# Two attention projections by Strassen's seven block products, with the banks, buffers and schedule around them rebuilt

## The reference, cut to what matters

```
q = xn @ wq            # 32 heads; of each head's 192 columns the first 128 are used
k = xn @ wkv[:, :32*128];  v = xn @ wkv[:, 32*128:64*128]
scores = where(causal, (q_h . k_h) * 192**-0.5, -1e30)     # per batch row, sequence 128 or 256
attn   = softmax(scores) @ v_h ;   x += attn.reshape(..) @ wo
x += xn @ W_base.T + b_base + experts(xn)
```

## Time and profile before

| | |
|---|---|
| median of 3 runs | 1168.38 us (1167.16 to 1169.59) |
| the profiled execution | 1166.81 us, span 1165.1 us |
| granted TensorE clock, mean over the span | 0.996 |
| VectorE busy | 514.5 us (44%), 1409 instructions |
| ScalarE busy | 402.9 us (35%) |
| GpSimd busy | 491.2 us (42%) |
| HBM read | 56.50 MB, 50 GB/s |

### The profile page before, as it was taken

How to read it: one execution, slowest core, us unless ns; L and a number is a source line. 1 busy time by engine, 2 the same in 40 slices (tenths; PEclk the granted TensorE clock), 3 DMA queues, 4 the chain that set the end, 5 groups by cost and what they waited for, 6 DMA issues and landing times.

```text
span 1165.1 us, 18048 instructions
## 1 busy us (share of the span) xinstructions
PE 1149.5 (99%) x6014; PEld 986.4 (85%) x6014; DVE 514.5 (44%) x1409; ACT 402.9 (35%) x1215; POOL 491.2 (42%) x623
## 2 busy tenths in 40 slices
PE   8989999999999999999999999999999999999998
PEld 7767888898888888888888888888888888888887
DVE  6776256275344334334433443344234423443345
ACT  2321132012363236224513451355135413532451
POOL 3655497671354136323623351346135512642330
PEclk9989999999999999999999999999999999999999
DMA  6312322130011002000200030112011100110001
GB/s 207 106 57 84 126 90 72 46 113 28 19 64 37 28 18 72 27 27 18 90 9 27 18 99 0 36 44 64 0 36 56 52 27 18 63 36 28 10 1 73
DMA packets 24814, 59.00 MB, mean 51 GB/s; under 512 B 3536, under 2 KB 3856, under 8 KB 24656
## 3 DMA queue, kind: packets, MB, share of 16 engines
q1 hardware_dynamic: 24784, 58.61, 15.6%
HBM read 56.50 MB, written 2.10 MB: 50 GB/s over the span
## 4 chain that ended last, share of the span: by engine, by line
PE 94%; DVE 4%; ACT 1%; issue 0%; DMA 0%; SPq 0%; POOL 0%; DVEq 0%; ACTq 0%; POOLq 0%
PE banks L100 28%; PE banks L102 28%; PE banks L101 28%; PE banks L1189 4%; PE banks L1204 2%; PE banks L1180 2%; DVE acc L1113 1%; PE banks L708 0%; DMA acc<-in_x 0%; DVE work L417 0%; PE banks L832 0%; DVE s L488 0%; DVE hT_lo L445 0%; DVE s L487 0%; DVE work L442 0%
## 5 line engine op out<-in xcount | busy, mean ns | idle before, releaser
L1003 POOL TENSOR_SCALAR prob<-prob,inv 128x128 f32<-128x128 f32 x128 | 48.0, 375 | 544.5 <-DVE inv L1090 544.5
L100 PE MATMUL banks<-xT_hi,wqk_hi 128*128 128x512 f32 x512 | 208.0, 406 | 0.0
L102 PE MATMUL banks<-xT_hi,wqk_lo 128*128 128x512 f32 x512 | 200.1, 391 | 0.0
L101 PE MATMUL banks<-xT_lo,wqk_hi 128*128 128x512 f32 x512 | 199.6, 390 | 0.0
L1062 ACT ACTIVATE prob<-prob,top 128x128 f32<-128x128 f32 (+1 forms) x256 | 114.6, 449 | 192.8 <-DVE top L1100 192.8
L102 PEld LDWEIGHTS banks<-xT_hi,wqk_lo 128*128 128x128 f32 x512 | 96.1, 188 | 21.5
L101 PEld LDWEIGHTS banks<-xT_lo,wqk_hi 128*128 128x128 f32 x512 | 96.5, 189 | 17.1
L100 PEld LDWEIGHTS banks<-xT_hi,wqk_hi 128*128 128x128 f32 x512 | 96.2, 188 | 16.8
L1033 DVE TENSOR_TENSOR kT_lo<-banks,kT_hi 128x512 fp32r<-128x512 f32 x64 | 44.3, 692 | 140.9 <-ACT kT_hi L1028 140.9
L100 PE MATMUL banks<-wv_hi,xT_hi 128*128 128x512 f32 x256 | 103.4, 404 | 0.0
L100 PE MATMUL banks<-wo_hi,oT_hi 128*128 128x512 f32 x256 | 101.6, 397 | 0.0
(11 more groups left out here) (225 smaller groups left out, 2488.6 us busy)
## 6 DMA issues: line engine op xcount, KB each, us to landing
wqk_stage<-in_w_qk SPq DMA_DIRECT2D x32, 512.0 KB, 3.3
gu_stage<-in_w_gu SPq DMA_DIRECT2D x22, 512.0 KB, 3.3
wvo_stage<-in_w_v SPq DMA_DIRECT2D x32, 256.0 KB, 2.6
wvo_stage<-in_w_o SPq DMA_DIRECT2D x32, 256.0 KB, 2.6
wd_stage<-in_w_down SPq DMA_DIRECT2D x22, 256.0 KB, 2.7
acc<-in_x SPq DMA_DIRECT2D x8, 256.0 KB, 4.8
out<-acc SPq DMA_DIRECT2D x8, 256.0 KB, 2.0
tab<-in_w_comb SPq DMA_DIRECT2D x1, 1300.0 KB, 6.2
```

The costliest lines, as they stand in the source:

```text
L100: nc.tensor.matmul(out, w_hi, x_hi, start=first, stop=False)
L101: nc.tensor.matmul(out, w_hi, x_lo, start=False, stop=False)
L102: return nc.tensor.matmul(out, w_lo, x_hi, start=False, stop=last)
L1003: nc.gpsimd.tensor_scalar(prob[:, i, 0:P], prob[:, i, 0:P], inv[:, i, 0:1], 1.0, ALU.mult, ALU.mult)
```

## The change

The weights of a head's queries and keys, side by side, are a matrix of 512 features by 256 columns; the tokens are 512 by 1024. Both are cut into 2 x 2 blocks (features in two halves; queries and keys; tokens in two halves) and the product is formed by Strassen's scheme in Winograd's form: seven block products instead of eight, each of 2 x 3 matmuls of 512 columns into one bank (`product`). So a head has 42 matmuls of 512 columns where it had 48.

What comes with it:
- Once, at the end of layer 0: sums and differences of the token blocks (`mix`, four VectorE instructions of 128x256 for each of four tiles), their hi (ScalarE, 128x1024, `mixed_evac`) and lo (GpSimd, 128x1024), and a copy `xh` of the first half's transposed tiles (ScalarE, four times). VectorE's `mix` of tile 2 waits for GpSimd's lo of tile 0 (two buffers), and `linear_add(3)` stands behind all four mixes. SP now issues the first two attention loads as soon as the convolution is done (`y_done`).
- For each head on GpSimd (`prepare`): the key weights times 8 (`K_UNIT`), four sums or differences (S1 to S4, 128x256) and seven splits of 128x256 (hi and lo), instead of four instructions of 128x512.
- For each head on VectorE (`combine`): seven additions of 128x512, each of one SBUF and one PSUM operand; four of them write back to their PSUM bank, from which ScalarE and VectorE then take hi, full copy and lo as before. ScalarE copies the first product out of PSUM (`copy_p1`).
- The copy v_full moves from VectorE to ScalarE.
- W covers two heads instead of four: twice the units of 6 matmuls, and 128 additions to `acc` in all where there were 72.
- Banks: four of the products rotate over banks 0 and 1, all else over 2, 6 and 3; the transposes of a pair go into its score bank. Buffers oT and wo hold two heads; alignment of some buffers is 512 bytes instead of 2048.
- The first group is written out as well as the last; the loop runs over six.
- Less runs ahead inside layer 0: six of head 0's seven products in place of Q, K and two V.

The diff, cut to its core (the lists that give the order, the preparation of the weights, the combination, and layer 0's end):

```diff
-GBANKS = 4
+P1, P6, P2, P7, P4, P5, P3 = range(7)
+EVACUATED = P2, P4, P5, P3
+def with_pairs(slots, first=False):
+    for p, fill in enumerate(slots):
+        older = [] if first and p == 0 else [p - 1]
+        steps += [("S", p)] + [("T", n) for n in older] + [("X", p)] + fill[:1] + [("R", p)] + fill[1:]
+        steps += [("O", n) for n in older]
+MIDDLE_SLOTS = [
+    [("L", 0, P5), ("P", 0, P3), ("V", 4), ("L", 0, P3), ("Y", 4), ("P", 1, P1), ("W", 0, 0)],
+    [("P", 1, P6), ("V", 5), ("P", 1, P2), ("W", 0, 1), ("L", 1, P2)],
...
+    [("W", 0, 4), ("W", 0, 5), ("L", 1, P5), ("P", 1, P3), ("W", 0, 6), ("W", 0, 7)]]
+INNER_SLOTS = [
+    [("P", 2, P1), ("L", 1, P3), ("P", 2, P6)],
+    [("P", 2, P2), ("L", 2, P2), ("P", 2, P7)]]
+OUTER_SLOTS = [
+    [("P", 2, P4), ("W", 1, 0), ("L", 2, P4), ("P", 2, P5), ("W", 1, 1)],
...
+    [("L", 2, P3), ("P", 3, P6), ("W", 1, 4), ("P", 3, P2)],
+    [("L", 3, P2), ("P", 3, P7), ("W", 1, 5), ("P", 3, P4)],
+    [("L", 3, P4), ("W", 1, 6), ("P", 3, P5)],
+    [("L", 3, P5), ("P", 3, P3), ("W", 1, 7)],
+    [("P", 4, P1), ("L", 3, P3), ("P", 4, P6)],
+    [("P", 4, P2), ("V", 8), ("L", 4, P2), ("P", 4, P7), ("Y", 8), ("V", 9)],
+    [("P", 4, P4), ("V", 10), ("L", 4, P4), ("P", 4, P5), ("Y", 10), ("V", 11)]]
+SPLITS = [
+    forms(1, [P2, "S4", P7, P4]),
+    forms(1, [P5, P3]) + forms(2, ["scale", "S1", P1]),
...
+    forms(2, [P4, P5]) + WV[0:2],
+    WO[0:2],
...
+        def mix(t):
+            b1, b2 = banks[:, D + t, 0:2 * P], banks[:, D + t, 2 * P:4 * P]
+            a1, a2 = xh[:, t, 0:2 * P], xh[:, t, 2 * P:4 * P]
+            dve.wait_ge(xh_done, t + 1)
+            if t >= 2:
+                dve.wait_ge(mixed_ready, t - 1)
+            link(nc.vector.tensor_tensor(t1, b1, a1, ALU.subtract))
+            link(nc.vector.tensor_tensor(t2, b2, t1, ALU.subtract))
+            nc.vector.tensor_tensor(t3, t2, a1, ALU.subtract)
+            nc.vector.tensor_tensor(t4, a2, t2, ALU.subtract).then_inc(x_mixed, 1)
...
-        for t in range(TH, NT):
-            xT_evac(NT + t, D + t - TH)
-        for n in range(2, TH):
-            linear_add(n)
+        for t in range(TH):
+            xT_evac(NT + TH + t, D + t)
+            mix(t)
+            if t % 2:
+                linear_add(2 + t // 2)
         gates(0)
...
-        ahead(0, 1)
+        ahead(0)
         gated_transposes(0)
-        ahead(1, 2)
+        ahead(1)
         experts(0)
         gated_transposes(1)
-        ahead(2, 3)
+        ahead(2)
         experts(1)
-        ahead(3, 4)
+        ahead(3)
...
+    def combine(dve, g, steps, h, i):
+        bank = turn_bank(steps, ("P", h, i))
+        dve.wait_ge(prod_done, products(g, h, i))
+        if i == P6:
+            dve.wait_ge(p1_copied, g * GH + h + 1)
+            nc.vector.tensor_tensor(u2[:, :], u3[:, :], bank, ALU.add).then_inc(mix_done, 1)
+        elif i == P2:
+            nc.vector.tensor_tensor(bank, u3[:, :], bank, ALU.add).then_inc(mix_done, 1)
...
+    def product(pe, g, h, i, bank):
+        pe.wait_ge(form_ready, g * (GH * NP) + h * NP + i + 1)
+        for c in range(FT):
+            ins = matmul3(nc, bank, form_hi[:, i, c], form_lo[:, i, c],
+                          right[0][:, k0 + c, cols], right[1][:, k0 + c, cols], c == 0, c == FT - 1)
+        ins.then_inc(prod_done, 1)
```

More of the change, by code:

```diff
@@ L98, in matmul3 @@
+LAST_SPLITS = [[task for task in slot if task[0] != "wv" and (task[0] == "wo" or task[1] < GH)] for slot in SPLITS]
+PIECES = WV[0:2] + WO[0:2] + WV[2:4] + WO[2:4]
+LAST_PIECES = WO
+RING = 2
+WARM_UP = 17, 10
 def matmul3(nc, out, w_hi, w_lo, x_hi, x_lo, first, last):
@@ new lines, in attention, with groups, head, products @@
+    late_wo = tT_hi[:, 0:PAIRED], tT_lo[:, 0:PAIRED]
+    def groups(eng, body):
+        body(0, FIRST)
+        with eng.Fori(1, NG - 1) as g:
+            body(g, MIDDLE)
+        body(NG - 1, LAST)
+    def head(g, h):
+        return g * GH + h
+    def products(g, h, i):
+        return g * (GH * NP) + h * NP + i + 1 + PROD0
+    def mixes(g, h, m):
+        return g * (GH * NM) + h * NM + m + MIX0
+    def pieces(g, i):
+        return g * len(PIECES) + i + 1 + KD
+    def w_count(g, steps, step):
+        before = 0 if steps is FIRST else g * (2 * NT) - NT
+        return before + adds(steps).index(step) + 1
@@ new lines, in turn_bank, with o_part @@
+    def turn_bank(steps, step):
+        long = is_long(step)
+        own, taken = turns(steps, long)
+        ring = LONG if long else SHORT
+        return banks[:, ring[(taken.index(step) - (len(taken) if steps is FIRST else own)) % len(ring)]]
+    def o_part(steps, n):
+        h, half = n // BATCH, n % BATCH // 2
+        cols = slice(half * HALF, (half + 1) * HALF)
+        if steps is LAST and h >= PAIRED:
+            return late_oT[0][:, h % PAIRED, cols], late_oT[1][:, h % PAIRED, cols]
+        return oT_hi[:, h % PAIRED, cols], oT_lo[:, h % PAIRED, cols]
@@ new lines, in split_piece, with gpsimd_ahead @@
+    def split_piece(pool, i, hi, lo, count):
+        nc.gpsimd.tensor_scalar(hi, wvo_stage[:, i % RING], 1.0, 1.0, ALU.mult, ALU.mult).then_inc(vo_hi_done, 1)
+        pool.wait_ge(vo_hi_done, count)
+        nc.gpsimd.tensor_tensor(lo, wvo_stage[:, i % RING], as_f32(hi), ALU.subtract).then_inc(vo_ready, 1)
+    def gpsimd_ahead(pool, part):
+        if part == 0:
+            for what in HEAD_BEGIN:
+                prepare(pool, 0, 0, what)
+            return
+        for what in HEAD_END:
+            prepare(pool, 0, 0, what)
```

716 lines of the change are left out of this document (437 added, 279 removed), and 11 rows, old and new, of tables (GROUP, LAST_GROUP, START).

## The result

The changed kernel takes **1159.41 us** (median of 4 runs, 1157.67 to 1159.94) where the kernel before takes 1168.68 beside it: a ratio of 0.9918, 95% interval 0.9906 to 0.9931. It is faster by 9.3 us; the forecast was 24.6. The profiled execution is that of 1157.67, its span 1155.8 us.

A forecast was written before the change was run, and what follows sets the result against it. TensorE, busy 99% of the span, was taken as the bound. Terms -43.7 + 5.6 + 11 + 1.5 + 1 = -24.6 us on 1166.8, or 1143.8 against the median of 1168.4; range 1133 to 1155.

The forecast's parts named there:

- over 17: Sign of a wrong prediction: the meeting of the layers costs under 6 or over 17 us.
- What is removed, and the prices added: 192 matmuls at 0.2275 us, 43.7 us off TensorE; added per group: VectorE 22.0 us, GpSimd to 77, ScalarE to 48.
- 0.8 us per group: Looped groups' short slots: late VectorE and GpSimd chains delay transposes, 0.8 us in each of seven groups, 5.6 in all.
- The clean case: Rival: bank and pair chains in groups fit as now, the layers' meeting costs 6 us; 1131 us, chance 0.22.
- steps 1 to 3: Where the layers meet: late biases, slow mixes and slow second gates make TensorE lose 9 to 14 us.
- I take 11: Where the layers meet: the value chosen for TensorE's waits, 11 us from a range of 9 to 14.
- step 1: Layers' meeting: GpSimd prepares six tasks of head 0 ahead of the four biases, which end at 246.4, not 242.1.
- the price of the mixes: Layers' meeting: 1.7 us per tile free, 2.6 beside GpSimd; linear_add(3) at about 257, TensorE loses 5.5 us.
- Step 3: Layers' meeting: second gates slow beside GpSimd, TensorE has 2.7 us of products as cover; it loses 3.4 to 8.3 us.
- I add 1.5 here: Layers' meeting: lower granted clock about and after gaps, 1.5 us, from 3.4 us seen at a 5.7 us gap.
- I add 1: Tail: W(2,0) waits 0.7 us for oT_lo(13), W(2,4) 0.1 for oT_lo(15); 1 us added.
- the case of late chains: Rival: 2.7 us lost per group and the full 14 + 1.5 + 1 elsewhere; 1160 us, chance 0.13.

The follow-up runs named there:

- experiment 11: Changed kernel with unused filler matmuls in TensorE's three gaps where the layers meet, no wait shortened: 1154.37 us, ratio 0.9878 to the kernel before.
- experiment 1: Changed kernel with the mixes' second term kept in PSUM, so no subtraction has two SBUF operands: 1157.3 us, ratio 0.9913 to the kernel before.
- Experiment 6: Changed kernel with P4 and P5 moved ahead of W units in slots 10 and 11: 1154.65 us, ratio 0.988 to the kernel before.
- experiment 3: Changed kernel with GpSimd waiting for the second gates before splitting wv and the next head's forms: 1154.07 us, ratio 0.9885 to the kernel before.
- experiment 8: Changed kernel with additions of linear results 2 and 3 ahead of mixes 1 and 2, ScalarE's gate copies likewise: 1155.32 us, ratio 0.9889.
- experiment 9: Changed kernel with the edits of experiment 1 and experiment 8 together: 1151.95 us, ratio 0.9857 to the kernel before.
- experiment 2: Changed kernel with products P6, P2, P7 and P4 issued before the experts instead of P6 alone: 1157.3 us, ratio 0.991 to the kernel before.
- experiment 4: Changed kernel with the last two pieces of wo split one slot earlier in the last group: 1155.54 us, ratio 0.9884 to the kernel before.
- experiment 10: The kernel before, unchanged, profiled once more: 1169.09 us in its one run.
- experiment 7: Changed kernel with per-head buffer alignment back from 512 to 2048 bytes: 1157.48 us, ratio 0.9911 to the kernel before.

## Why the forecast was wrong

The mechanisms were those of the forecast, and the sign. The price of the layers' meeting was too small, 12.5 us for 20.5, in its waits as well as in its clock, and so was that of the tail, 1 for 5.6. The meeting is also past the forecast's own sign of being wrong, "over 17".

| term | forecast | measured |
|---|---|---|
| fewer matmuls | -43.7 | -43.7 |
| seven groups | 5.6 | 6.2 |
| waits where the layers meet | 11 (9 to 14) | 13.3, and 1.15 before the first scores; 16.3 with the clock held full (experiment 11) |
| clock behind them | 1.5 | 5.8; of these, 4.1 came back with the clock held full |
| tail | 1 | 5.6 |
| first layer | 0 | 2.0 |
| sum | -24.6 | -9.65 by the parts, -9.3 by the spans |

- **What is removed, and the prices added:** right (0.69 for a combination, 0.74 and 0.41 on GpSimd for 0.73 and 0.48). The rule quoted from the Trainium skill (GPSIMD Engine Reference, the table of specifications), contention with two SBUF inputs, agrees with experiment 1: the same subtraction took 1.3 to 2.6 us with both operands in SBUF beside GpSimd, and 0.42 with one in PSUM.
- **0.8 us per group:** right in size (0.86), and half wrong in place. I had T(11) late by 0.35 and T(12), T(13), T(6) by 0.1 to 0.2 each; the trace has one visible gap of 0.62 at T(11). Experiment 6 shows that it was a matter of order alone: a looped group loses nothing with P4 and P5 ahead of the W units (106.03 for 105.99). The clean case for the groups was within reach.
- **The layers' meeting, steps 1 to 3, "I take 11": right in kind, and the largest miss.** The trace after begins the meeting 2.0 us later. Less these 2.0, step 1's biases came at 241.7 to 247.2 for 241 to 246.4, nearly right, but linear_add(3) at 259.6 for 257. The step that failed is the price of the mixes and of what stands behind them: the four took 13.6 us for four times 2.6, since a stretched instruction took up to 2.57 and not some 0.9; linear_add(2) itself stands behind mix(1); and ScalarE's copy, behind its rounding, costs each addition 1.30 more. Units 4 and 5 lost 8.8 at full clock (6.4 in the trace, where the slow unit 4 hides the rest) for 5.5. Step 3's gap is 6.9 (6.5 in experiment 11), inside 3.4 to 8.3, and the 1.15 before the first scores were not in the sum. Experiments 3, 8 and 9 take single causes away; with experiment 2 they speak for VectorE's chain as the bound between them.
- **"I add 1.5 here", the clock: the step that failed beside it.** I took 0.19 and 0.15 of 10 us from the earlier trace rows and halved them, once, for a gap of 5.7 us. In the trace after, each of three gaps has its own slow stretch, 2.25, 1.56 and 2.03 us of extra time behind it. By the rows that I had, a gap costs up to 3.4 us beside its length; with three gaps forecast (before units 4 and 5 and before the experts) that was up to 10, and 1.5 stood at the bottom of it. Experiment 11 gives the price apart from the waits: 4.1 us of the 5.8 come back with every wait left in place; the rest lay in unit 4 and was slack, since VectorE sets the start of unit 5. So of the 8.0 us that the meeting cost beyond the forecast, 2.6 were the clock and 5.4 the waits (as the trace shows them, 4.3 and 3.5).
- **Tail, "I add 1": the third.** I followed W(2,0) to oT_lo(13), and not to the last pieces of wo. GpSimd splits them behind the scaling of pair 14, until 1138, and TensorE stands 2.96 us; experiment 4 took it away. GpSimd's queue in that group was not followed at all. 0.46 and 0.48 stand before two scores; 1.7 of the 5.6 has no gap that I could name, and stays open.
- **First layer:** by experiment 10 no part of the change. Both kernels have starts that differ by 2 us from trace to trace (239.01 and 241.26, 241.01 and 239.33). Without it the changed kernel's profiled execution would have been 11 us faster than the one before.
- **Rivals.** The measured time, 1159.4, lies beside the case of late chains (1160), but by luck and not for its reason, 2.7 us per group; most of the time went before and behind the groups. The alignment of the buffers is out (experiment 7).

## What to carry to other kernels

Work taken off the bounding engine was paid for at its seams here: look where two stages meet and at the last group for work that the other engines must now do first, follow each of their queues by hand to the last instruction, and price each gap of TensorE at its length plus the slow stretch behind it, once per gap. Where an engine's queue is the bound, one edit may only move the wait (1, 2 and 8 did, 3 did not); judge such edits together too. In an order written out by hand, look at what stands between a late engine's last input and the instruction that needs it: two pieces of work exchanged gave 0.82 us a group.
